# A normalised group is scaled one turn later in ScalarE's order, behind the copy of a further input group

## The chip, the cores and the metric

The kernel runs on one core of one Trainium2 chip. The metric is the device time of one execution in microseconds (us). A core has five engines that run their own instruction queues and meet at semaphores: TensorE (PE), VectorE (DVE), ScalarE (ACT), GpSimd (POOL) and SyncE (SP, which only issues transfers here). The time before is 3870.34 us, the median of three runs.

## What is computed

Two transformer layers with adaptive layer norms on x of 16 sequences x 256 tokens x 128 features, in f32. Cut to its frame, the reference is:

```python
# layer 0
h = _layernorm(x) * (1 + ca) + sa
x = x + ga * _L0_attn_ref(h, ...)        # linear attention and an MLP of 512
h = _layernorm(x) * (1 + cb) + sb
x = x + gb * _L0_ffn_ref(h, ...)         # six layers of local attention and gated MLP
# layer 1
h = _layernorm(x) * (1 + ca) + sa
x = x + ga * _L1_attn_ref(h, ...)        # causal multi-query attention with a relative bias
h = _layernorm(x) * (1 + cb) + sb
x = x + gb * _L1_ffn_ref(h, ...)         # MLP of 512
```

where `_layernorm` is `(x - m) / sqrt(v + eps)` over the 128 features, and the scales, shifts and gates (`ca`, `sa`, `ga` and so on) are one value per sequence and feature, from a small product at the start. The change touches the four lines with `_layernorm` and nothing else.

## The kernel before, in words

x is held transposed (features on partitions, `xT`, 128 x 4096), and so is the normalised result (`yT`). The program is a chain of stages with a barrier of all engines behind each. Four of the stages are calls of `layernorm_modulate`, tagged n0, n1, n2 and n3. Each works on 8 groups of 512 tokens. For one group the work goes round all engines:

- **front**, the copy in. In n1, n2 and n3 ScalarE copies the group from `xT` to `src` (L266), and TensorE transposes it into a bank of the four-deep ring `TA` (L190, four 128 x 128 transposes), so that tokens are on partitions. In n0 the input comes from memory into `src` by a transfer (L170); TensorE transposes that, and ScalarE copies `TA` to `xT` (L270).
- **stats**: VectorE takes sums (L217) and means and variances (L222); GpSimd makes `rstd` from them (L249, L251).
- **norm**: VectorE subtracts and multiplies (L229) into `xn`, two deep.
- **back**: TensorE transposes `xn` into `TB`, two banks (L197), and ScalarE applies scale and shift per sequence, in two instructions of 256 columns, into `yT` (L275). This pair on ScalarE is what is called **out** below; its semaphore is `out_done`.
- **residual**, in n2 only: VectorE adds the gated result of the stage before to `xT` (L236), and ScalarE's copy of the group waits for that.
- **split**: GpSimd makes high and low parts of the next stage's weights, beside the rest: two instructions in each of six turns in n1 (L480, L482), one in some turns of n3 (L1829 to L1839) and of n2 (L2108 to L2120).
- **swap**, in n2 only and for groups 4 to 7: TensorE multiplies two pieces of the relative bias by a matrix (L2087) into two spare banks, and ScalarE takes them out in four copies (L2098, L2099).

What sets the order is one table, `LN_ORDER`, from which every engine spells its own queue: in turn t, each engine does those of its steps that the table names, in the table's order, each for group t minus the step's lag. No engine can pass a step of its own that waits. Before, ScalarE's turn t is front of group t, then out of group t-3, then swap of group t-1; TensorE's is front t, back t-3, swap t-1; VectorE's residual t, norm t-3, stats t-1; GpSimd's stats t-1, split t-3.

The waits that matter for the change are those of the rings:

```python
ring_wait(pe, normed, u, 1, LN_RING)   # L186: front of u waits for norm of u-4
pe.wait_ge(normed, u.count(1, 1))      # L194: back of u waits for norm of u
ring_wait(pe, out_done, u, SPG)        # L195: and for out of u-2
ring_wait(dve, back_done, u, 1)        # L227: norm of u waits for back of u-2
ring_wait(act, turned, u, 1, LN_RING)  # L265: the copy of u waits for front of u-4
act.wait_ge(back_done, u.count(1, 1))  # L273: out of u waits for back of u
```

In n2, a swap product on TensorE also waits until the spare bank's copies of two products before are out, and the copies wait for the product.

Of the kernel before, what the change touches and what calls it, by code (L numbers as in the profile page):

```python
# [121 lines left out]
def ring_wait(eng, sem, grp, per, lag=2):  # L122

    if grp.at >= lag or grp.loop is not None:
        eng.wait_ge(sem, grp.count(per, per, lag))


LN_ORDER = [("residual", 0), ("front", 0), ("norm", 3), ("stats", 1), ("back", 3), ("swap", 1), ("split", 3)]
LN_RING = 4


def spelled(order, steps, n=NGRP):


    for t in range(n + max(lag for _, lag in order)):
        for name, lag in order:
            if name in steps and 0 <= t - lag < n:
                steps[name](Group(t - lag))


def layernorm_modulate(nc, tag, g, dst, scale, bias, from_dram=None, residual=None, load=None, split=None, swap=None):


    with ExitStack() as ctx:
# [13 lines left out]
        turned, stats, aggr, varp, rstd_done, normed, back_done, out_done, x_done, res_done = map(sem, (  # L158
            "turned", "stats", "aggr", "varp", "rstd_done", "normed", "back_done", "out_done", "x_done", "res_done"))
        per_src = 16 if from_dram is not None else 1  # L160
        with nc.Block() as block:
            if from_dram is not None:
                @block.sync
                def _(sp):
                    tokens = from_dram.rearrange("b (t p) f -> p (b t) f", p=128)

                    def front(u):
                        ring_wait(sp, normed, u, 1, LN_RING)
                        ring_wait(sp, turned, u, 1, LN_RING)
                        sp.dma_start(src[:, u.at % LN_RING], tokens[:, u.at * TPG:(u.at + 1) * TPG, :]).then_inc(src_ready[u.at % LN_RING], 16)  # L170
                        if load:
                            load(sp, u.at)

                    spelled(LN_ORDER, {"front": front})
            elif load:
# [6 lines left out]
            def _(pe):  # L182
# [18 lines left out]
                if swap:  # L201
                    steps["swap"] = lambda u: swap.multiply(pe, spare, u.at)
                spelled(LN_ORDER, steps)

            @block.vector
            def _(dve):
# [34 lines left out]
                if residual is not None:  # L241
                    steps["residual"] = add_residual
                spelled(LN_ORDER, steps)

            @block.gpsimd
            def _(pool):
# [8 lines left out]
                if split:  # L255
                    steps["split"] = lambda u: split(pool, u.at, out_done)
                spelled(LN_ORDER, steps)

            @block.scalar
            def _(act):  # L260
                def front(u):
                    if from_dram is None:
                        if residual is not None:
                            act.wait_ge(res_done, u.count(1, 1))
                        ring_wait(act, turned, u, 1, LN_RING)  # L265
                        nc.scalar.activation(src[:, u.at % LN_RING].rearrange("p t f -> p (t f)"), g.xT[:, u.cols()],  # L266
                                             ACT.Copy).then_inc(src_ready[u.at % LN_RING], 1)
                    else:
                        act.wait_ge(turned, u.count(1, 1))
                        nc.scalar.activation(g.xT[:, u.cols()], TA[u.at % LN_RING][:, :], ACT.Copy).then_inc(x_done, 1)  # L270

                def back(u):
                    act.wait_ge(back_done, u.count(1, 1))  # L273
                    for q in range(SPG):
                        nc.scalar.activation(dst[:, u.cols(q * SEQ, SEQ)], TB[u.par][:, q * SEQ:(q + 1) * SEQ],  # L275
                                             ACT.Identity, bias=bias[:, u.seq(q)],
                                             scale=scale[:, u.seq(q)]).then_inc(out_done, 1)

                steps = {"front": front, "back": back}
                if swap:  # L280
                    steps["swap"] = lambda u: swap.evict(act, spare, u.at)
                spelled(LN_ORDER, steps)

# [1514 lines left out]
class NetworkWeights:  # L1798
# [25 lines left out]
    def split(self, pool, n, out_done):  # L1824

        nc = self.nc
        if n == 1:
            pool.wait_ge(self.loaded, 16 * (3 + MCH))
            nc.gpsimd.tensor_tensor(self.w1p[0][:, :], self.w1[:, :], self.zero.broadcast_to((128, MLP)), ALU.add).then_inc(self.w1_split, 1)  # L1829
        if n == 2:  # L1830
            pool.wait_ge(self.w1_split, 1)
            nc.gpsimd.tensor_tensor(self.w1p[1][:, :], self.w1[:, :], self.w1p[0][:, :].bitcast(F32),
                                    ALU.subtract).then_inc(self.w1_split, 1)
        if n == 3:
            nc.gpsimd.tensor_tensor(self.w2p[0][:, :, :], self.w2[:, :, :], self.zero.unsqueeze(2).broadcast_to((128, MCH, D)),
                                    ALU.add).then_inc(self.w2_split, 1)
        if n == 4:
            pool.wait_ge(self.w2_split, 1)
            nc.gpsimd.tensor_tensor(self.w2p[1][:, :, :], self.w2[:, :, :], self.w2p[0][:, :, :].bitcast(F32),  # L1839
                                    ALU.subtract).then_inc(self.w2_split, 1)  # L1840
# [722 lines left out]
```

## Time and profile before

| | us |
|---|---|
| median of three runs (3863.09 to 3870.75) | 3870.34 |
| the profiled execution, its own time | 3875.89 |
| its span in the trace | 3874.0 |
| stage n0, first transfer to last out | 19.5 to 43.0 |
| stage n1, first copy to last out | 216.4 to 246.6 |
| stage n2, first residual to last out | 3306.1 to 3339.5 |
| stage n3, first copy to last out | 3787.0 to 3814.5 |

The four stages together are about 115 us of 3874. In rows of a timeline, the columns are start, duration, engine, line, operation, output and inputs, shapes and count of the merged instructions, and in brackets how long the engine had been idle before and what released it. PEclk, the granted TensorE clock, is given as a share of the full 2.4 GHz; 0.50 is 1.2 GHz.

### The profile page before, as it was taken

How to read it: one execution, taken by the hardware profiler on the slowest of the kernel's cores; microseconds unless marked ns; L12 is line 12 of the kernel's file. 1: busy time of each engine (PE TensorE's matmuls, PEld its weight loads, DVE VectorE, ACT ScalarE, POOL GpSimd, SP SyncE). 2: the span in 40 equal slices, each digit the busy share in tenths (PEclk: the TensorE clock that was granted, in tenths of full speed). 3: DMA queues.
4: the chain of work that ended last, by engine and by line, in shares of the span. 5: the costliest groups of instructions: out<-in, count | busy, mean ns of one | idle time of the engine just before them, and what ended most of it. 6: DMA issues, size and time to landing. Idle time of an engine off the chain costs nothing. (4 is left out here: it accounts for less than half of the span.)

```text
span 3874.0 us, 189325 instructions
## 1 busy us (share of the span) xinstructions
PE 3676.6 (95%) x70910; PEld 2945.0 (76%) x70910; DVE 3136.4 (81%) x9407; ACT 2884.3 (74%) x8517; POOL 2453.3 (63%) x2556
## 2 busy tenths in 40 slices
PE   7869999999999999999999999999999999899997
PEld 4558888688886788876888868888688886466665
DVE  7878888688887788877888878888788887666667
ACT  4758888478885788865888758888478885677775
POOL 3657777377774677756777647777377773454553
PEclk9979999999999999999999999999999999899998
DMA  1013333233332233332333323333233331100000
GB/s 48 1 52 82 80 81 83 58 81 81 81 81 71 72 82 80 82 83 58 82 81 81 89 52 80 81 81 81 60 81 81 80 81 45 36 1 0 0 0 28
DMA packets 305289, 245.99 MB, mean 63 GB/s; under 512 B 74485, under 2 KB 299860, under 8 KB 304340
## 3 DMA queue, kind: packets, MB, share of 16 engines
q1 hardware_dynamic: 305108, 243.72, 24.9%
q8 instruction: 96, 1.57, 0.2%
q14 instruction: 85, 0.70, 0.1%
HBM read 24.54 MB, written 2.12 MB: 7 GB/s over the span
## 5 line engine op out<-in xcount | busy, mean ns | idle before, releaser
L1220 POOL TENSOR_TENSOR wa_t<-wa_t,wa_rn 128x512 f32<-128x512 f32 x768 | 785.3, 1043 | 280.5 <-DVE wa_rn L1048 277.1
L880 ACT ACTIVATE wa_pb<-wa_sc,wa_nm 128x64 f32<-128x64 f32 x3072 | 670.1, 329 | 367.4 <-DVE wa_nm L1070 336.3
L1226 POOL TENSOR_TENSOR wa_t<-wa_t 128x512 f32<-128x512 f32 x384 | 496.1, 1292 | 413.2 <-DVE wa_t L1024 413.2
L1022 DVE TENSOR_TENSOR wa_t<-wa_pj,wa_ctab 128x512 f32<-128x512 f32 x768 | 528.0, 688 | 213.2 <-PE wa_ta L624 168.0
L45 PE MATMUL wa_pj<-lw_wqkv_high,wa_xhigh 128*128 128x512 f32 x1152 | 533.2, 463 | 37.4 <-DVE wa_t L1024 19.2
L863 ACT ACTIVATE wa_sq<-wa_pj 128x512 f32<-128x512 f32 x768 | 487.0, 636 | 61.5 <-PE wa_pj L47 59.5
L1235 POOL TENSOR_TENSOR wa_t<-wa_t 128x512 f32<-128x512 f32 x384 | 490.2, 1276 | 0.0
L47 PE MATMUL wa_pj<-lw_wqkv_high,wa_xlow 128*128 128x512 f32 x1152 | 461.2, 400 | 0.0
L46 PE MATMUL wa_pj<-lw_wqkv_low,wa_xhigh 128*128 128x512 f32 x1152 | 458.2, 398 | 1.2 <-issue 1.2
L1030 DVE TENSOR_REDUCE wa_raw<-wa_sq 128x16 f32<-128x1024 f32 x384 | 449.3, 1170 | 0.0
L683 PE MATMUL wa_ob<-wa_oT,lw_wo 128*128 128x128 f32 x3120 | 420.3, 278 | 3.1 <-DVE wa_on L1082 3.0
L743 PE MATMUL wa_ob<-wa_vv,wa_pT 64*32 64x65 f32 x24576 | 387.3, 227 | 26.5 <-issue 23.9
L683 PEld LDWEIGHTS wa_ob<-wa_oT,lw_wo 128*128 128x128 f32 x3120 | 383.3, 193 | 7.9 <-issue 6.2
L743 PEld LDWEIGHTS wa_ob<-wa_vv,wa_pT 64*32 64x32 f32 x24576 | 316.6, 105 | 38.3 <-issue 29.9
L2190 POOL TENSOR_TENSOR mq_pb<-mq_pb,mq_rs 128x256 f32<-128x256 f32 (+1 forms) x256 | 206.1, 826 | 219.7 <-DVE mq_rs L2335 219.7
L730 PE MATMUL wa_sc<-wa_kT,wa_qT 64*32 64x64 f32 x24576 | 329.6, 223 | 1.8 <-issue 1.6
L1024 DVE TENSOR_TENSOR wa_t<-wa_pj,wa_stab 128x256 f32<-128x256 f32 x768 | 318.9, 415 | 0.0
L1023 DVE TENSOR_TENSOR wa_t<-wa_pj,wa_stab 128x256 f32<-128x256 f32 x768 | 318.8, 415 | 0.0
L730 PEld LDWEIGHTS wa_sc<-wa_kT,wa_qT 64*32 64x32 f32 x24576 | 301.7, 105 | 2.8 <-issue 2.2
L1070 DVE TENSOR_REDUCE wa_nm<-wa_sc 128x8 f32<-128x512 f32 x384 | 265.6, 692 | 45.7 <-PE wa_sc L730 22.2
L45 PEld LDWEIGHTS wa_pj<-lw_wqkv_high,wa_xhigh 128*128 128x128 f32 x1152 | 217.6, 189 | 108.5 <-DVE wa_t L1024 31.3
L1082 DVE TENSOR_TENSOR wa_on<-wa_ob,wa_rs 128x512 f32<-128x512 f32 x384 | 261.8, 682 | 1.5
(287 smaller groups left out, 8633.4 us busy)
## 6 DMA issues: line engine op xcount, KB each, us to landing
wa_vv<-wa_vt SPq DMA_DIRECT2D x2304, 65.0 KB
wa_vv<-wa_vt SPq DMA_DIRECT2D x1152, 32.5 KB
lw_wqkv<-L_ffn_Wqkv SPq DMA_DIRECT2D x6, 1536.0 KB, 6.1
lw_xs<-yT SPq DMA_DIRECT2D x96, 64.0 KB, 1.9
lw_fs<-yT SPq DMA_DIRECT2D x48, 128.0 KB
lw_xs<-yT SPq DMA_DIRECT2D x96, 63.8 KB, 1.9
lw_fs<-yT SPq DMA_DIRECT2D x96, 63.8 KB
lw_wo<-L_ffn_Wo SPq DMA_DIRECT2D x6, 512.0 KB, 4.2
```

The lines of the kernel that those rows point to most:

```text
L45: nc.tensor.matmul(out, lhs[0], rhs[0], start=start, stop=False)
L46: nc.tensor.matmul(out, lhs[0], rhs[1], start=False, stop=False)
L47: return nc.tensor.matmul(out, lhs[1], rhs[0], start=False, stop=stop)
L683: last = nc.tensor.matmul(OB[:, 0, Y0:Y0 + 128], wo[:, PR * h + j, :], oT[:, u.tile(5), PR * h + j, :], start=(j == 0), stop=(j == PR - 1) ...
L730: last = nc.tensor.matmul(SC[q, e, p * KEYS:(p + 1) * KEYS], qT[r, u.par(2), p, q], kT[r, h2, p, k0:k0 + KEYS], start=False, stop=True, sk ...
L743: last = nc.tensor.matmul(OB[q, e, p * VW:(p + 1) * VW], pT[r, u.par(3), p, q], vv[r, u.ring(3), n, p, :], start=True, stop=True, skip_gro ...
L863: nc.scalar.activation(sq[:, j * HG:(j + 1) * HG, :], PJ[j][:, :].rearrange("p (h d) -> p h d", h=HG), ACT.Square).then_inc(s.sq_done, 1)
L880: last = nc.scalar.activation(pb[:, u.par(2), p, e, :], SC[:, e, p * KEYS:(p + 1) * KEYS], ACT.Exp, bias=nm[:, u.par(2), e, p:p + 1])
L1022: nc.vector.tensor_tensor(t1[:, b, j], x, table(ctab, slice(0, HD)), ALU.mult)
L1220: nc.gpsimd.tensor_tensor(here, here, rn[:, u.par(1), j * HG:(j + 1) * HG].unsqueeze(2).broadcast_to((128, HG, HD)), ALU.mult).then_inc(s. ...
L1226: nc.gpsimd.tensor_tensor(t1[:, b, 0], t1[:, b, 0], t2[:, b, 0], ALU.add).then_inc(s.qadd_done, 1)
L1235: nc.gpsimd.tensor_tensor(t1[:, b, 1], t1[:, b, 1], t2[:, b, 1], ALU.add).then_inc(s.kadd_done, 1)
```

## The change

Two lines: the table gets an eighth entry, `("out", 4)`, behind split, and ScalarE registers its function `back` under that name rather than under `"back"`. TensorE keeps `"back"` at lag 3.

```diff
-LN_ORDER = [("residual", 0), ("front", 0), ("norm", 3), ("stats", 1), ("back", 3), ("swap", 1), ("split", 3)]
+LN_ORDER = [("residual", 0), ("front", 0), ("norm", 3), ("stats", 1), ("back", 3), ("swap", 1), ("split", 3), ("out", 4)]
 LN_RING = 4
...
-                steps = {"front": front, "back": back}
+                steps = {"front": front, "out": back}
                 if swap:
                     steps["swap"] = lambda u: swap.evict(act, spare, u.at)
                 spelled(LN_ORDER, steps)
```

The queues of TensorE, VectorE, GpSimd and SyncE stay row for row as they were. ScalarE's turn t becomes front of t, swap of t-1, out of t-4. The first place is ScalarE in n3 (n1 is alike, and n0 too with the line L270 for L266), from the first copy on; `n_src<-xT` is the copy in, `yT<-n_tb` the out pair:

```order
 L259 UNCONDITIONAL_BRANCH
-L266 ACTIVATE n_src<-xT 128x512 x4
+L266 ACTIVATE n_src<-xT 128x512 x5
 L275 ACTIVATE yT<-n_tb,mod 128x256 x2
 L266 ACTIVATE n_src<-xT 128x512
```

Five copies stand ahead of the first out pair, where four did; from there the two alternate, and the last five pairs stand behind the last copy, where four did (x10 for x8).

The second place is ScalarE in n2, in the turns with swap; `mq_bias<-n_spare` are the copies of the relative bias. Before, from the copy of group 6 to that of group 7 and the pair behind it:

```order
L266 ACTIVATE n_src<-xT 128x512
L275 ACTIVATE yT<-n_tb,mod 128x256 x2
L2098 ACTIVATE mq_bias<-n_spare 128x2x128
L2099 ACTIVATE mq_bias<-n_spare 128x2x256
L2098 ACTIVATE mq_bias<-n_spare 128x2x128
L2099 ACTIVATE mq_bias<-n_spare 128x2x256
L266 ACTIVATE n_src<-xT 128x512
```

And now the same turn:

```order
L266 ACTIVATE n_src<-xT 128x512
L2098 ACTIVATE mq_bias<-n_spare 128x2x128
L2099 ACTIVATE mq_bias<-n_spare 128x2x256
L2098 ACTIVATE mq_bias<-n_spare 128x2x128
L2099 ACTIVATE mq_bias<-n_spare 128x2x256
L275 ACTIVATE yT<-n_tb,mod 128x256 x2
L266 ACTIVATE n_src<-xT 128x512
```

The pair moved from ahead of the four copies to behind them, and it is the pair of group 2, where it was that of group 3.

## Rows read from the trace of the kernel before

**Rows 1.** The page's first line.
```profile
span 3874.0 us, 189325 instructions
```
**Rows 2.** Timeline of ScalarE at the end of stage n0.
```profile
38.07 0.60 ACT L270 ACTIVATE xT<-n_ta 128x512 f32<-128x512 f32 x1 [1.14 <-PE n_ta L190]
38.56 2.91 ACT L275 ACTIVATE yT<-n_tb,mod 128x256 f32<-128x256 f32 x6
41.97 1.02 ACT L275 ACTIVATE yT<-n_tb,mod 128x256 f32<-128x256 f32 x2 [0.50 <-PE n_tb L197]
```
**Rows 3.** Timeline of GpSimd in stage n1, one turn of six.
```profile
234.41 0.20 POOL L249 TENSOR_TENSOR n_rstd<-n_mv,eps 128x4 f32<-128x4 f32 x1
...
236.80 1.27 POOL L482 TENSOR_TENSOR lw_wqkv_low<-lw_wqkv,lw_wqkv_high 128x512 fp32r<-128x512 f32 x1
238.03 0.20 POOL L249 TENSOR_TENSOR n_rstd<-n_mv,eps 128x4 f32<-128x4 f32 x1
```
**Rows 4.** Timeline of VectorE at the end of stage n1.
```profile
242.97 1.37 DVE L229 TENSOR_SCALAR n_xn<-n_ta,n_mv,n_rstd 128x128 f32<-128x128 f32 x4 [2.25 <-POOL n_rstd L251]
```
**Rows 5.** Timeline of ScalarE in stage n3, one turn of four.
```profile
3803.18 0.62 ACT L266 ACTIVATE n_src<-xT 128x512 f32<-128x512 f32 x1
3805.86 1.02 ACT L275 ACTIVATE yT<-n_tb,mod 128x256 f32<-128x256 f32 x2 [2.06 <-PE n_tb L197]
3806.78 0.62 ACT L266 ACTIVATE n_src<-xT 128x512 f32<-128x512 f32 x1
```
**Rows 6.** Timeline of VectorE in stage n3: stats of groups 3, 4 and 7, last norms.
```profile
3796.24 0.89 DVE L217 BATCH_NORM_STATS2 n_st<-n_ta 128x6 f32<-128x128 f32 x4
...
3798.71 0.88 DVE L217 BATCH_NORM_STATS2 n_st<-n_ta 128x6 f32<-128x128 f32 x4
...
3808.61 0.89 DVE L217 BATCH_NORM_STATS2 n_st<-n_ta 128x6 f32<-128x128 f32 x4 [1.04 <-PE n_ta L190]
...
3809.84 2.85 DVE L229 TENSOR_SCALAR n_xn<-n_ta,n_mv,n_rstd 128x128 f32<-128x128 f32 x8
```
**Rows 7.** Timeline of GpSimd in stage n3, the last `rstd`.
```profile
3810.28 1.01 POOL L251 TENSOR_TENSOR n_rstd<-n_rstd,mhalf 128x4 f32<-128x4 f32 x1
```
**Rows 8.** Timeline of ScalarE in stage n2, copies of groups 5 to 7 and the end.
```profile
3319.65 0.62 ACT L266 ACTIVATE n_src<-xT 128x512 f32<-128x512 f32 x1
...
3326.50 0.63 ACT L266 ACTIVATE n_src<-xT 128x512 f32<-128x512 f32 x1
3328.32 1.02 ACT L275 ACTIVATE yT<-n_tb,mod 128x256 f32<-128x256 f32 x2 [1.19 <-PE n_tb L197]
3329.24 0.38 ACT L2098 ACTIVATE mq_bias<-n_spare 128x256 f32<-128x256 f32 x1
...
3330.80 0.63 ACT L266 ACTIVATE n_src<-xT 128x512 f32<-128x512 f32 x1
...
3337.47 1.99 ACT L275 ACTIVATE yT<-n_tb,mod 128x256 f32<-128x256 f32 x4
```
**Rows 9.** Timeline of TensorE and VectorE in stage n2.
```profile
3327.19 0.66 PE L190 MATMUL n_ta<-ident,n_src 128*128 128x128 f32 x4 [1.48 <-ACT n_src L266]
...
3328.12 1.88 PE L2087 MATMUL n_spare<-mq_hank,mq_swap 128*128 128x512 f32 x4
...
3318.08 0.85 DVE L236 SCALAR_TENSOR_TENSOR xT<-yT,mod,xT 128x256 f32<-128x256 f32 x2
```
**Rows 10.** Line L2087 over the whole run, duration in ns min/median/max.
```profile
L2087 PE MATMUL n_spare<-mq_hank,mq_swap x16: 592/592/1057, 3322.1 to 3335.9; 128*128 128x512 f32 x16
```
**Rows 11.** Timeline of TensorE in n0, behind a wait of 2.41 us.
```profile
29.30 1.12 PE L190 MATMUL n_ta<-ident,n_src 128*128 128x128 f32 x4 [2.41 <-DMA n_src<-L_attn_x]
```
**Rows 12.** Stretches of the span: length, busy time of each engine, PEclk, DMA share, GB/s.
```profile
28.00:30.00 2.00, 0.69 (x3) 0.70 (x4) 1.96 (x14) 0.00 (x0) 1.01 (x3) 0.70 0.45 94
...
3330.00:3332.00 2.00, 0.52 (x6) 0.52 (x6) 0.45 (x2) 1.43 (x4) 1.56 (x2) 1.00 0.02 4
...
3812.00:3814.00 2.00, 0.66 (x4) 0.42 (x4) 0.68 (x3) 1.51 (x4) 0.00 (x0) 1.00 0.00 0
```

## The prediction

> **What bounds the kernel now.** I read the page first, for the size of what is touched, then the timeline of each engine through the four stages, and last the granted clock in stretches of them. The page gives a span of 3874.0 us [rows 1]; the profiled execution took 3875.89 us by its own time, 1.9 us more than the span and 5.6 us above the median of 3870.34. The four stages of `layernorm_modulate` are 115 us of that, each closed by a barrier, so what a stage gains or loses at its last out pair goes one to one into the time, and nothing done earlier inside a stage counts. Each has another bound:
>
> *n0* is held by VectorE and the loads until the end. In its tail ScalarE runs three out pairs back to back and then waits 0.50 us for the last group [rows 2]: little slack is left there.
>
> *n1* is held by GpSimd. One turn there takes 238.03 - 234.41 = 3.62 us, and no row has idle time in front of it [rows 3]. The last norm waits 2.25 us for GpSimd's `rstd`, and the last out pair follows that norm [rows 4].
>
> *n3* is held by a loop of ScalarE and TensorE: out of group u, behind it the copy of group u+4, its transposes, then the back transposes of u+1, then out of u+1. The turn is 3806.78 - 3803.18 = 3.60 us, with 2.06 us of ScalarE waiting in it [rows 5]. VectorE, when not held, needs 3798.71 - 3796.24 = 2.47 us a turn; late in the stage it waits 1.04 us a turn for TensorE [rows 6]. That n1 and n3 both show 3.6 us is chance: in n1 GpSimd's two splits a turn make it, and the loop happens to be as long.
>
> *n2* has the same loop until group 5. Then it has bias products too: 3330.80 - 3326.50 = 4.30 us from copy to copy [rows 8].
>
> **The change, part by part.** No instruction is added or removed; only ScalarE's order differs. Since nothing is added, each price is a difference in when the last out pair ends.
>
> *n0: +0.4 us.* Five pairs now stand behind the last copy in place of four. The pairs take (2.91 - 1.02) / 2 = 0.95 us each from start to start. The last copy is released by TensorE, as before. So the fifth pair starts at 38.56 + 4 x 0.95 = 42.36, against 41.97 [rows 2]. The back transposes wait for the pair of two groups before: that of group 3 ends at about 39.6, four transposes take 0.66 [rows 9], and the pair of group 5 is not due before 40.46; so for groups 6 and 7 too, some 0.2 us apart. ScalarE alone sets this. The loads do not see the change; if they did, a late one could cost some tenths more.
>
> *n1: 0.* ScalarE's and TensorE's work moves earlier, up to VectorE's norms, which wait for GpSimd. GpSimd waits for nobody in turns 4 to 8, so the last norm stays at 242.97 and the last pair where it is [rows 3, 4]. The cover is GpSimd's splits; without them this stage would behave as n3. Bounds: -0.5 and +0.5, for the clock of the last transposes.
>
> *n3: -2.5 us.* The copy of group u+4 no longer stands behind out of u, so TensorE finds its input ready and the loop is open: back transposes of u+1 need norm u+1 and out of u-1, and both are there. Next late is VectorE. From its stats of group 4 on it can keep 2.47 us a turn: stats of group 7 at 3798.71 + 3 x 2.47 = 3806.12 rather than 3808.61 [rows 6]. Its norm then waits for `rstd`, which ended 3810.28 + 1.01 = 3811.29, that is 2.68 us behind the start of those stats [rows 7]: 3808.80, and with the same 1.37 us as in n1 [rows 4] norm ends at 3810.2, where before the norms ended at 3809.84 + 2.85 = 3812.69. GpSimd has at most 1.27 us of split a turn here beside 1.3 us of `rstd`, 2.5 in all, which about fits. I take -2.5; if GpSimd is a little too long, -2.0; if the last two transposes run at the other clock, 0.5 off either way (1.12 against 0.66 us for four [rows 9, 11]).
>
> *n2: +4.9 us.* Here the pair does not only move behind the next copy, it moves behind the bias copies of its turn, and these wait for TensorE's products of the same turn. TensorE's back transposes of group t-3 stand ahead of those products and wait for out of t-5. So the pair, the copy of the next group, its transposes, the back transposes, the products and the bias copies come to stand in one line, where before the pair ran beside the products. The turn, at full clock: copy to first product 3328.12 - 3326.50 = 1.62 [rows 8, 9]. A product is two pieces, and four pieces take 1.88 us, the last 0.59 [rows 9, 10], so a piece is 0.43 from start to start and the first product is out 0.43 + 0.59 + 0.02 = 1.04 behind its start, the second 0.86 later. The second bias copy pair follows that and takes (3330.80 - 3329.24) / 2 = 0.78; the out pair takes 3329.24 - 3328.32 = 0.92 [rows 8]. Sum 1.62 + 1.04 + 0.86 + 0.78 + 0.92 = 5.22 against 4.30.
> Ahead of that, the copy of group 5 is freed from the pair and starts behind its residual, at 3318.08 + 0.85 + 0.04 = 3318.97 instead of 3319.65, which brings the turn forward by 0.68 [rows 8, 9]; but out of group 1 (0.92) now stands ahead of the copy of group 6: +0.24, at 3326.74. Copy of group 7: 3331.96. Out of group 3 starts 4.30 later, 3336.26, and is done at 3337.32; only then come back transposes of 5 and, 0.43 on, the last products; their copies start at 3338.8 and 3339.65, out of group 4 at 3340.4, and three more pairs at 0.95 behind it: the last starts at 3343.3 and ends at 3344.3, against 3337.47 + 1.99 = 3339.46 [rows 8]. That is +4.9.
>
> *The clock in n2.* In the new turn of 5.22 us TensorE works for 3328.12 - 3327.19 = 0.93 of transposes and 1.88 of products, and waits for 2.41 us, where it was 1.48 [rows 9]. Before, the clock stayed at 1.00, the 2.4 GHz level, over those waits [rows 12]. In n0 a wait of 2.41 us was followed by transposes at 1.12 us for four, and the clock of that stretch was 0.70, so it had fallen to the 1.2 GHz level [rows 11, 12]. A turn at the low level costs 2 x (1.12 - 0.66) + 4 x (1.057 - 0.592) = 2.8 us more [rows 9, 10, 11]. I take none for the forecast, since the products keep TensorE busier than n0's transposes did; one to three such turns are rivals.
> The Trainium skill (TensorE: Matmul & The Clock Gate, HAM oscillation) says that waits between short bursts throw the clock back, so that each next burst starts slow; by it the sum would have 2.8 us more per turn. The row of n0 agrees, the rows of n2 before do not yet show it.
> Stages n1 and n3 are almost all transposes, and n3's last ones ran at 1.00 [rows 12]. The same page (Part 4: PE-mode transpose) says that transposes do not raise the clock; the trace speaks against it here, and by it n2 would hang on the products alone and fall more easily.
>
> **The sum:** 0.4 + 0 + 4.9 - 2.5 = +2.8 us, or 3875.89 + 2.8 = 3878.7 for the profiled execution and 3873.1 for the median. That is 0.07%.
>
> **The rivals.**
> *A, the clock falls in one or two turns of n2* (0.20 and 0.10). For it: the longer wait and n0's row. Against: n2's turns hold 1.88 us of products each. It gives +5.6 or +8.4: 3875.9 or 3878.7, the second just past 0.2%.
> *B, the clock stays low from the first product turn of n2 to the end* (0.06). Three turns, 8.4 us: +11.2, or 3881.5, slower by 0.29%. It decides if the clock does not rise around 3326, as it did before, or falls at once. Against: the first products run without a gap, as before.
> *C, the wait for out of t-5 does not bind in n2* (0.09), because TensorE runs ahead: n2 then costs at most the 0.92 of a pair, and the net is 0.4 - 2.5 + 0.92 = -1.2 or less: 3869. Against: the queue order allows TensorE no step past back transposes.
> *D, n1 gains too* (0.03): if GpSimd's busy rows had slack that the timeline hides, six turns could fall from 3.6 towards 2.5: -6 more, 3867. Against: VectorE waits for exactly that engine.
> That the change does not do what it says is excluded: the order shows it, and only on ScalarE.
>
> **How the numbers follow.** The forecast has 0.52, the rivals the rest. What a measurement of this kernel can tell from no change is about 0.2%, 7.7 us; the three runs before alone differ by that much. Forecast, C, D and one slow turn all lie within it; slower needs B or two slow turns, and the spread of runs: 0.13. Faster by more than 7.7 us comes from no case but the spread: 0.03. The range runs from 3867 (D, or C with the spread) to 3881 (A, nearly B); the likeliest case alone, with the bounds of its terms, is 3871 to 3876.
>
> **What would show it.** In the profile of the changed kernel: in n3 stats of the last groups 2.5 us apart with no wait for TensorE, and the stage ending 2.5 us sooner against its first copy; in n1 a last pair at the same distance from the first copy, 30.2 us; in n0 five pairs in a row; in n2 out pairs behind the bias copies, copies of groups 6 and 7 5.2 us apart and TensorE waiting about 2.4 us ahead of its transposes, the stage 38 us long for 33.4. Wrong would be: a shorter n2, a wait for `rstd` gone in n1, or a difference outside these stages.

## The result, and the profile after

The changed kernel takes 3878.83 us, the median of eight runs (3873.01 to 3884.7); the kernel before takes 3870.8 us over its eight runs of the same comparison. The ratio is 1.0020, with a 95% interval of 1.0012 to 1.0029: 8.0 us slower, between 4.6 and 11.2. That is inside the range (3867 to 3881 us), well above the forecast (+2.8) and close to rival A with two slow turns (+8.4). It is just past the 0.2% that I had called the limit of what can be told.

The profiled execution after took 3873.01 us by its own time, with a span of 3871.2 us, 2.8 us *shorter* than the one before. The two spans must not be compared: the local attention between n1 and n2, which no edit touches, took 3059.5 us there and 3050.2 us here. The stages themselves can be compared, since each begins behind a barrier (one execution each; run 4 shows how far a stage can differ from one execution to the next):

| stage, from where to where | before | after | forecast | 
|---|---|---|---|
| n0, last input copy to end of last out pair | 4.92 | 6.20 | +0.4 |
| n1, first copy to end of last out pair | 30.19 | 30.18 | 0 |
| n2, the same | 32.48 | 40.49 | +4.9 |
| n3, the same | 27.45 | 25.13 | -2.5 |
| sum of differences | | +7.0 | +2.8 |

Timeline of ScalarE after, in n2, which answers to [rows 8]:

```profile
3319.35 0.65 ACT L266 ACTIVATE n_src<-xT 128x512 f32<-128x512 f32 x1
3322.46 0.39 ACT L2098 ACTIVATE mq_bias<-n_spare 128x256 f32<-128x256 f32 x1 [2.46 <-PE n_spare L2087]
...
3324.16 0.39 ACT L2098 ACTIVATE mq_bias<-n_spare 128x256 f32<-128x256 f32 x1 [0.83 <-PE n_spare L2087]
...
3324.92 1.03 ACT L275 ACTIVATE yT<-n_tb,mod 128x256 f32<-128x256 f32 x2
3325.82 0.65 ACT L266 ACTIVATE n_src<-xT 128x512 f32<-128x512 f32 x1
```

The wait has moved. Before, ScalarE waited 1.19 us in such a turn, for the back transposes. Now it waits 2.46 us and then 0.83 us for the products, and the out pair stands behind both. From copy to copy the turn is 6.47 us where it was 4.30, and where 5.22 was forecast at the high clock. TensorE in the same stretch:

```profile
3320.05 0.66 PE L190 MATMUL n_ta<-ident,n_src 128*128 128x128 f32 x4 [2.40 <-ACT n_src L266]
3320.55 0.60 PE L197 MATMUL n_tb<-ident,n_xn 128*128 128x128 f32 x4
3320.99 3.14 PE L2087 MATMUL n_spare<-mq_hank,mq_swap 128*128 128x512 f32 x4
3326.52 0.66 PE L190 MATMUL n_ta<-ident,n_src 128*128 128x128 f32 x4 [2.40 <-ACT n_src L266]
...
3331.30 0.71 PE L197 MATMUL n_tb<-ident,n_xn 128*128 128x128 f32 x4 [1.97 <-ACT yT L275]
3331.82 3.53 PE L2087 MATMUL n_spare<-mq_hank,mq_swap 128*128 128x512 f32 x4
```

The wait ahead of the transposes is 2.40 us, for a forecast of 2.41. The row of 3331.30 shows the link on which the sum rested: back transposes waiting 1.97 us for an out pair (L275). But the four pieces of the products took 3.14 us in this turn and 3.53 us in the last, where [rows 9] has 1.88. The clock fell while they ran, as stretches of the span show (length, busy time of each engine, PEclk, DMA share, GB/s):

```profile
3320.00:3322.00 2.00, 1.95 (x10) 1.41 (x11) 1.35 (x11) 0.00 (x1) 0.99 (x1) 0.87 0.00 0
3322.00:3324.00 2.00, 2.00 (x3) 0.33 (x1) 1.31 (x5) 0.87 (x2) 1.78 (x3) 0.50 0.00 0
3324.00:3326.00 2.00, 0.12 (x1) 0.00 (x0) 0.00 (x0) 1.84 (x5) 0.43 (x1) 0.78 0.01 4
3326.00:3328.00 2.00, 1.48 (x10) 1.24 (x11) 0.78 (x4) 0.47 (x1) 0.00 (x0) 1.00 0.00 0
...
3332.00:3334.00 2.00, 2.00 (x4) 0.83 (x3) 1.36 (x4) 0.23 (x1) 0.00 (x0) 0.50 0.00 0
```

0.87, 0.50, 0.78, 1.00 and again 0.50: the clock goes down to the 1.2 GHz level and up to 2.4 GHz from turn to turn. Before, it rose once, behind the first product turn (its four pieces took 3.62 us in both kernels), and then stayed up through the stage; [rows 12] has a stretch of that.

Timeline of VectorE after in n3, which answers to [rows 6]:

```profile
3795.09 0.88 DVE L217 BATCH_NORM_STATS2 n_st<-n_ta 128x6 f32<-128x128 f32 x4
...
3797.55 0.88 DVE L217 BATCH_NORM_STATS2 n_st<-n_ta 128x6 f32<-128x128 f32 x4
...
3800.01 0.88 DVE L217 BATCH_NORM_STATS2 n_st<-n_ta 128x6 f32<-128x128 f32 x4
...
3804.95 0.88 DVE L217 BATCH_NORM_STATS2 n_st<-n_ta 128x6 f32<-128x128 f32 x4
...
3807.66 1.37 DVE L229 TENSOR_SCALAR n_xn<-n_ta,n_mv,n_rstd 128x128 f32<-128x128 f32 x4 [0.17 <-POOL n_rstd L251]
```

Stats are 2.46 us apart to the end with no wait for TensorE, and the last norm waits 0.17 us for `rstd`, as worked out.

In n1 the second, third and fourth out pair come sooner after the first copy than before; the last five start 3.61 us apart, GpSimd's pace. The row that answers to [rows 4], VectorE:

```profile
244.95 1.36 DVE L229 TENSOR_SCALAR n_xn<-n_ta,n_mv,n_rstd 128x128 f32<-128x128 f32 x4 [2.24 <-POOL n_rstd L251]
```

With the first copy at 218.36 that is 26.59 us into the stage; before it was 242.97 - 216.38 = 26.59.

The tail of n0 after, ScalarE first, to be held against [rows 2], then TensorE and VectorE:

```profile
38.78 0.60 ACT L270 ACTIVATE xT<-n_ta 128x512 f32<-128x512 f32 x1 [1.73 <-PE n_ta L190]
39.27 1.93 ACT L275 ACTIVATE yT<-n_tb,mod 128x256 f32<-128x256 f32 x4
41.56 1.94 ACT L275 ACTIVATE yT<-n_tb,mod 128x256 f32<-128x256 f32 x4 [0.35 <-PE n_tb L197]
43.96 1.02 ACT L275 ACTIVATE yT<-n_tb,mod 128x256 f32<-128x256 f32 x2 [0.46 <-PE n_tb L197]
```
```profile
40.44 2.00 PE L197 MATMUL n_tb<-ident,n_xn 128*128 128x128 f32 x8 [0.84 <-ACT yT L275]
42.80 1.12 PE L197 MATMUL n_tb<-ident,n_xn 128*128 128x128 f32 x4 [0.37 <-DVE n_xn L229]
```
```profile
41.63 1.12 DVE L229 TENSOR_SCALAR n_xn<-n_src,n_mv,n_rstd 128x128 f32<-128x128 f32 x4 [0.81 <-PE n_tb L197]
```

It had been forecast that the five pairs run in one piece. They do not; there are two waits between them. Read from the end: the last pair waits for the last transposes, these for norm of group 7, this for back transposes of group 5 (L227, the ring of `xn`), and these, from 40.44, for out of group 3. The transposes took 1.12 us for four here; before they took 0.66 us in this tail.

### The profile page after: what moved, and what is told of

Same layout as the page of the kernel before. It is cut to its first block and busy times, and to the rows that moved or that the text cites. A ratio compares the mean times of both kernels' runs of the same rounds, so it can differ in the third digit from the quotient of the medians.

```text
span 3871.2 us, 189325 instructions
## 1 busy us (share of the span) xinstructions
PE 3673.9 (95%) x70910; PEld 2938.1 (76%) x70910; DVE 3133.8 (81%) x9407; ACT 2890.6 (75%) x8517; POOL 2454.3 (63%) x2556
```

## The experiments

In all kernels below the table is chosen per stage, with `OLD` as before and `NEW` as in the change:

```diff
+LN_NEW = [("residual", 0), ("front", 0), ("norm", 3), ("stats", 1), ("back", 3), ("swap", 1), ("split", 3), ("out", 4)]
+LN_OLD = [("residual", 0), ("front", 0), ("norm", 3), ("stats", 1), ("back", 3), ("out", 3), ("swap", 1), ("split", 3)]
```

Stage lengths of n1 to n3 are from the first copy to the end of the last out pair; times of kernels are medians against the kernel before on the same chip.

**1. Out at lag 4, but ahead of swap.**

```diff
-... ("back", 3), ("swap", 1), ("split", 3), ("out", 4)]
+... ("back", 3), ("out", 4), ("swap", 1), ("split", 3)]
```

> All four stages keep out at lag 4, but it stands ahead of swap in the order instead of at its end; only stage n2 differs from the change by that. My theory (in n2 the loss comes from the out pair standing behind the bias copies, which wait for TensorE's products, which stand behind back transposes that wait for an out pair): n2 goes back to 33 to 34 us from 41.4, out pairs run at once behind the copy of their turn, n3 stays at 25.1 us and n1 at 30.2; over before n0 +0.4 to +2, n2 0 to +0.5, n3 -2.3, sum 0 to -2 us. Rival 1 (lag 4 as such costs n2, since pairs pile up at the end, wherever they stand in a turn): n2 stays at 38 us or more and the kernel at +5 us. Rival 2 (the loss is outside the four stages): the kernel stays at +8 us although n2 is short.

Measured: n2 is 33.29 us, n3 24.82, n1 30.18, n0 6.20 from its last copy. The kernel: 3868.09 us, ratio 1.0000 (0.9991 to 1.0009). ScalarE's timeline, to be compared with the one above:

```profile
3321.14 0.63 ACT L266 ACTIVATE n_src<-xT 128x512 f32<-128x512 f32 x1
3321.66 1.02 ACT L275 ACTIVATE yT<-n_tb,mod 128x256 f32<-128x256 f32 x2
...
3325.43 0.63 ACT L266 ACTIVATE n_src<-xT 128x512 f32<-128x512 f32 x1
```

The pair goes out at once behind the copy, and copies are 4.29 us apart. All but 0.8 of n2's 8.0 us hangs on which side of the bias copies the pair stands; both rivals fall. With n2 back, what is left of the stages nearly cancels, and so does the kernel's time.

**2. The new order in n2 alone.** `order=LN_NEW` for n2, `LN_OLD` for the others.

> The new order in stage n2 alone, the old one in n0, n1 and n3. My theory: n2 is 38.3 us long with TensorE's clock at 1.00 throughout its product turns, 2.8 us more for each product turn at 0.50, so 38 to 44 us against 33.4; the kernel is +5 to +9 us against before, which is more than the whole change made only if the gain of n3 (2.3 us) is real. Rival 1 (n0 brings half of the loss): +4 us or less. Rival 2 (the loss is outside the stages): nothing within the stage but a few us.

Measured: n2 43.02 us, 10.5 us over the 32.48 of before (six profiles of n2 in the old order lie between 32.29 and 33.07); 3875.66 us, ratio 1.0022 (1.0013 to 1.0031), +8.5 us. Copies of groups 6 and 7 are 6.89 us apart. This one stage carries the whole loss.

**3. The same, with TensorE's waits partly filled.**

```diff
-steps["swap"] = lambda u: swap.multiply(pe, spare, u.at)
+steps["swap"] = lambda u: (swap.multiply(pe, spare, u.at), [nc.tensor.transpose(TA[(u.at + 2) % LN_RING][:, 0:D], g.ident[:, :], g.ident[:, :]) for _ in range(10 if u.at >= 4 else 0)])
```

> As the run with the new order in n2 alone, but behind the products of each of the four product turns TensorE does ten more 128x128 transposes of the identity into a bank that is free, about 1.1 us at the high clock, inside the 2.4 us for which it waits there. They add nothing that anyone reads. My theory of a loss of two parts: the waits let the clock fall, so with them partly filled the clock stays at 1.00 from the first product turn's end, every later turn is 5.2 us from copy to copy, and n2 is 38 to 39 us; the kernel +4 to +6 us against before. If the clock has no part in the loss: n2 as long as in that run, or longer by the fillers. If it is all clock: n2 back to 33 to 34 us.

Measured: n2 37.84 us; 3874.15 us, ratio 1.0014 (1.0005 to 1.0023). TensorE's timeline (L202 are the added transposes) and ScalarE's copies:

```profile
3324.52 1.88 PE L2087 MATMUL n_spare<-mq_hank,mq_swap 128*128 128x512 f32 x4
3326.24 1.25 PE L202 MATMUL n_ta<-ident 128*128 128x128 f32 x10
3328.80 0.66 PE L190 MATMUL n_ta<-ident,n_src 128*128 128x128 f32 x4 [1.30 <-ACT n_src L266]
3329.29 0.60 PE L197 MATMUL n_tb<-ident,n_xn 128*128 128x128 f32 x4
3329.73 1.88 PE L2087 MATMUL n_spare<-mq_hank,mq_swap 128*128 128x512 f32 x4
```
```profile
3322.89 0.65 ACT L266 ACTIVATE n_src<-xT 128x512 f32<-128x512 f32 x1
...
3328.10 0.65 ACT L266 ACTIVATE n_src<-xT 128x512 f32<-128x512 f32 x1
```

Products at 1.88 us in every turn but the first, a turn of 5.21 us against 5.22 forecast: more work on TensorE, and the stage is 5.2 us shorter. So of run 2's 10.5 us in n2, about half is the longer line (5.4 us, run 3 against before) and about half the clock (5.2 us, run 2 against run 3). That is read from one profile of each. The kernels' medians are only 1.5 us apart, with intervals of the ratio that overlap (1.0022 and 1.0014), so what the clock costs on average of the executions is not shown, and is likelier less than 5.2 us.

**4. The changed kernel once more.**

> The changed kernel once more, for a second look at its clock. My theory: in n2 each product turn is 5.2 us from copy to copy with the transposes at 0.66 us and the products at 1.88 us, and up to 2.8 us longer where they run at the low clock, so n2 is 37.8 to 43 us from the first copy, wherever the fall comes; n3 25 us, n1 30.2 us, n0 6.2 us from its last copy. Rival (n2's length has nothing to do with the clock): 40.5 us again with other speeds of the transposes.

Measured: n2 43.08 us, n3 24.95, n1 30.20, n0 6.20; one run of 3879.65 us. TensorE in n2:

```profile
3324.22 2.86 PE L2087 MATMUL n_spare<-mq_hank,mq_swap 128*128 128x512 f32 x4
3329.48 1.04 PE L190 MATMUL n_ta<-ident,n_src 128*128 128x128 f32 x4 [2.39 <-ACT n_src L266]
...
3331.17 2.81 PE L2087 MATMUL n_spare<-mq_hank,mq_swap 128*128 128x512 f32 x4
3335.94 0.64 PE L197 MATMUL n_tb<-ident,n_xn 128*128 128x128 f32 x4 [1.97 <-ACT yT L275]
3336.41 3.58 PE L2087 MATMUL n_spare<-mq_hank,mq_swap 128*128 128x512 f32 x4
```

The waits (2.39, 1.97) are as before, and the stage is 2.6 us longer than in the first profile of this kernel. Only half of that is the clock. From the copy of group 5 to the end of the stage it is 29.81 us, and it was 28.51; there the clock fell in three turns and not in two. The other 1.3 us lie ahead of that copy (13.27 us from the first copy, and it was 11.98), and most of them are this: GpSimd's first split starts when its weights have arrived, and here it ran beside VectorE's residual of group 5, which then took 1.69 us. In the first profile that residual took 0.85 us, and the overlap came with group 6's, off the line:

```profile
3310.71 0.85 DVE L236 SCALAR_TENSOR_TENSOR xT<-yT,mod,xT 128x256 f32<-128x256 f32 x2
```

and in this one, VectorE and GpSimd:

```profile
3313.12 1.69 DVE L236 SCALAR_TENSOR_TENSOR xT<-yT,mod,xT 128x256 f32<-128x256 f32 x2
3313.09 1.04 POOL L2108 TENSOR_TENSOR mq_wq_high<-mq_wq,zero 128x512 fp32r<-128x512 f32 x1 [1.52 <-DMA mq_bout<-L_attn_bout]
```

Runs 2 and 3 have that overlap too (13.23 and 13.16 us to the copy of group 5), so the comparison between them stands. In all three profiles of n2 in this order without fillers (40.5, 43.0, 43.1 us) the clock fell in at least two turns.

**5. The new order in n3 alone.**

> The new order in stage n3 alone. My theory: n3 is 25.1 us long, first copy to end of last out pair, against 27.45 before, VectorE's stats 2.47 us apart; the kernel gains 2.3 us, of which three rounds may not tell much. Rival (n3's length moves with the clock, not with the order): 25 to 27.5 us with turns of 3.6 us left in it.

Measured: n3 25.01 us, stats 2.46 to 2.47 us apart; 3865.41 us, ratio 0.9995 (0.9986 to 1.0004), which can't be told from 1. Over all the runs here, n3 is 26.87 to 27.48 us in the old order (eight profiles) and 24.82 to 25.18 us in the new one (five profiles).

**6. The new order in n1, with GpSimd relieved.** The first of the two splits is made by ScalarE:

```diff
-        pool.wait_ge(lw.w_loaded, 48)
-        nc.gpsimd.tensor_tensor(hi[:, here], full[:, here], zero.broadcast_to((128, WCOLS)), ALU.add).then_inc(lw.w_first, 1)
+        act.wait_ge(lw.w_loaded, 48)
+        nc.scalar.activation(hi[:, here], full[:, here], ACT.Copy).then_inc(lw.w_first, 1)
```

as a step `("high", 3)` of ScalarE, behind back and, in this order, ahead of out; GpSimd's second split then waits for it.

> Stage n1 alone has the new order, and GpSimd's cover there is halved: the first of its two splits a turn (adding zero and rounding) is made by ScalarE as a copy, behind the front copy of its turn. n0, n2 and n3 have the old order. My theory (n1 showed nothing because GpSimd's 3.6 us a turn hid the opened loop): GpSimd needs 2.5 us a turn now, the loop is open, and n1 falls from 30.2 to 24.5 us; the kernel gains 5.6 us. Rival (the loop of ScalarE and TensorE holds n1 whatever GpSimd does): n1 stays above 29 us.

Measured: n1 24.49 us; 3862.29 us, ratio 0.9985 (0.9976 to 0.9994), -5.8 us. GpSimd's timeline, one turn:

```profile
232.39 0.20 POOL L249 TENSOR_TENSOR n_rstd<-n_mv,eps 128x4 f32<-128x4 f32 x1
...
233.64 1.27 POOL L491 TENSOR_TENSOR lw_wqkv_low<-lw_wqkv,lw_wqkv_high 128x512 fp32r<-128x512 f32 x1
234.87 0.19 POOL L249 TENSOR_TENSOR n_rstd<-n_mv,eps 128x4 f32<-128x4 f32 x1
```

2.48 us a turn, where [rows 3] has 3.62: with the cover gone the opened loop is worth 5.7 us in n1.

**7. The same relief, in the old order.** `("out", 3)` ahead of `("high", 3)`.

> As the run with the new order in n1 and the split's first half on ScalarE, but with the old order in n1 too. My theory: with out ahead of the next copy the loop is closed, and the extra copy on ScalarE stands in it: about 4.15 us a turn, n1 31.6 us long against 30.2, the kernel +1.5 us. Rival (relieving GpSimd is what gains, the order has no part in it): n1 at 25 to 27 us here too.

Measured: n1 30.92 us, 3869.21 us, ratio 1.0004 (0.9994 to 1.0013). ScalarE:

```profile
232.53 1.02 ACT L275 ACTIVATE yT<-n_tb,mod 128x256 f32<-128x256 f32 x2 [2.06 <-PE n_tb L197]
233.44 0.62 ACT L482 ACTIVATE lw_wqkv_high<-lw_wqkv 128x512 fp32r<-128x512 f32 x1
...
236.65 1.02 ACT L275 ACTIVATE yT<-n_tb,mod 128x256 f32<-128x256 f32 x2 [2.06 <-PE n_tb L197]
```

4.12 us a turn, and the same 2.06 us of waiting in it. Relief and order are worth nothing apart and 5.7 us together.

**8. In n2, the bias copies a turn later too.** ScalarE takes the products of a turn out in the next one:

```diff
-... ("back", 3), ("swap", 1), ("split", 3), ("out", 4)]
+... ("back", 3), ("out", 4), ("swap", 1), ("unswap", 2), ("split", 3)]
...
-                    steps["swap"] = lambda u: swap.evict(act, spare, u.at)
+                    steps["unswap"] = lambda u: swap.evict(act, spare, u.at)
```

> In stage n2 alone: out at lag 4 ahead of the bias copies, and the bias copies on ScalarE at lag 2, one turn behind TensorE's products, so that they never wait for products of the same turn. Others old. My theory of one long line in n2: with the bias copies out of it too the stage is 29 to 31 us from the first copy, against 32.4 before and 40.5 with the change, and the kernel gains 2 to 4 us. Rival (ScalarE's and TensorE's work as such fills the product turns): n2 stays at 32 us or more.

Measured: n2 29.30 us, 3863.81 us, ratio 0.9987 (0.9978 to 0.9996), -5 us, where the stage gives -3.2 and the interval reaches from -8.5 to -1.5. Copies of groups 5, 6 and 7 are 3.26 and 3.25 us apart, at VectorE's pace.

**9. The new order in n0 alone.**

> The new order in stage n0 alone. From the last input copy to the end of the last out pair: 4.9 us before and in three runs with the old order there, 6.2 us in both runs with the new one, where the transposes of the tail ran at 1.12 us for four. My corrected theory: the back transposes of group 5 wait for out of 3, norm of 7 for those, and the last two transposes and the pair for that, so the stage's tail depends on the transposes: 5.3 us if they take 0.66 us, 6.2 us if 1.12 us. Rival (ScalarE's five pairs alone, as forecast): 5.3 us at either.

Measured: 6.19 us from the last copy, with transposes at 1.12 us for four (one execution, 3872.56 us, which says nothing at this size). The low clock alone does not make it: in five of the runs with the old order in n0 (2, 3, 5, 6 and 7) the last input's transposes also took 1.11 or 1.12 us, and the tail was 4.83 to 4.96 us all the same. In run 2, for example, TensorE's rows are

```profile
37.57 1.11 PE L190 MATMUL n_ta<-ident,n_src 128*128 128x128 f32 x4 [1.80 <-DMA n_src<-L_attn_x]
38.48 1.91 PE L197 MATMUL n_tb<-ident,n_xn 128*128 128x128 f32 x8
```

Old order and slow transposes, and no wait between groups 4 and 5; and behind these the transposes of groups 6 and 7 got faster again, down to 0.66 us in runs 3 and 6. In all four profiles of the new order without fillers, the transposes of groups 5 to 7 took 1.12 us to the end of the stage, even in run 4, where the last input's had taken 0.66 us. So the slow tail goes with the new order here; that the new order causes it is not shown. How the old order does with a slow tail to the end, no run shows, so how much of the 1.3 us is the order's and how much the clock's is bounded only by the next run.

**10. The same, with fillers in n0's waits.**

```diff
+LN_RING = 4; FILL = {2: 2, 3: 6, 4: 3}
...
                     last.then_inc(back_done, 1)
+                    if from_dram is not None and u.at in FILL:
+                        pe.wait_ge(x_done, 5)
+                        for t in range(FILL[u.at]):
+                            nc.tensor.transpose(TA[0][:, 0:D], g.ident[:, :], g.ident[:, :])
```

> The new order in n0 alone, with 2, 6 and 3 transposes of the identity into a free bank behind the back transposes of groups 2, 3 and 4, inside TensorE's waits, so that its clock may be high in the tail. If the last transposes then take 0.66 us for four: my corrected chain (last copy, out of 3, back of 5, norm of 7, back of 7, out of 7) gives 0.5 + 1.05 + 0.7 + 1.15 + 0.7 + 1.05 = 5.2 to 5.3 us from the last copy, against 6.2 in four runs with slow ones and 4.9 with the old order. If they stay at 1.12 us: 6.2 again, and the fast case stays unseen. Rival (the tail is 6.2 us whatever the transposes take): 6.2 at 0.66 us too.

Measured: 5.28 us (one execution, 3869.97 us). ScalarE, where L274 and L279 are the lines L270 and L275 of before:

```profile
37.74 0.60 ACT L274 ACTIVATE xT<-n_ta 128x512 f32<-128x512 f32 x1 [1.36 <-PE n_ta L190]
38.24 4.78 ACT L279 ACTIVATE yT<-n_tb,mod 128x256 f32<-128x256 f32 x10
```

With the transposes at 0.66 us the five pairs run in one piece, as the forecast had them, and the tail is 0.4 us longer than in the old order. The last two transposes were just in time, so both the chain and ScalarE's own work give that figure.

**11. What the runs favour in each stage, together.** n0 as before, n1 as in run 6, n2 as in run 8, n3 as in the change.

> Each stage with what the runs so far favour: n0 the old order; n1 the new one with the split's first half on ScalarE; n2 out at lag 4 ahead of the bias copies and these at lag 2; n3 the new order. If the stages add up, as they must with a barrier behind each: n1 24.5, n2 29.3, n3 25.0 us, so -5.7 - 3.1 - 2.3 = -11 us against before, some 0.29%. If a stage's length leans on the one before it (the clock that is handed over): -7 to -9 us.

Measured: 3857.82 us against 3867.8, ratio 0.9974 (0.9964 to 0.9983), 10 us faster than before and 18 us faster than the change by the two ratios. n1 24.55, n2 29.06, n3 25.18 us: the stages give 5.6 + 3.4 + 2.3 = 11.3 us, and the interval reaches from 6.6 to 13.9, so they add up within it.

## Why the prediction was right in kind and short in size

- *n1: 0.* Right to 0.01 us, and for the reason given: run 6 takes the cover away and the gain appears (24.49 us).
- *n3: -2.5.* -2.3 in the first profile, about -2.1 between the medians of all profiles. VectorE is next late, as forecast.
- *n2: +4.9, the line.* The mechanism was right link by link: the pair behind the bias copies (run 1 undoes just that), the turn of 5.22 us (5.21 in run 3), the wait of 2.41 us (2.40), and ahead of it a copy of group 5 that comes 0.69 us sooner after the first copy, for 0.68 forecast (in runs 2, 3 and 4 VectorE's slow residual hides that). The line alone measures 5.4 us in run 3, 4.9 of them behind the copy of group 5, where the forecast had 5.5; its first products took 2.95 us for 3.62 before, which is the difference.
- *n2, the clock.* Here is the step that failed: "I take none for the forecast, since the products keep TensorE busier than n0's transposes did". n0's row with a wait of 2.41 us and a fallen clock [rows 11, 12] was the nearest evidence for a wait that I had worked out at 2.41 us, and I set it aside for an argument with no row behind it. Clock falls came in all three profiles, and from the copy of group 5 on the stage is 3.8 to 5.1 us longer than run 3. Rival A had the right mechanism, at a chance of 0.30 that looks low now, but not the right sizes: the falls came in two or three turns, and such a turn is 1.3 to 1.7 us longer than run 3's 5.21 (6.47, 6.89 and 6.88 us), not 2.8, because the low level held for a part of the turn only. The Trainium skill cited there (TensorE: Matmul & The Clock Gate, HAM oscillation) describes such a clock for bursts that are shorter than the waits between them. In the trace of the change PEclk is 1.00 and 0.50 in turn, with products at 1.88 and 3.53 us, although TensorE's 2.8 us of work were longer than its wait of 2.40; and it is not as the page has it that the next burst starts slow, since the transposes ahead of the slow products still took 0.66 us (in run 4 they took 1.04).
- *n0: +0.4.* "ScalarE alone sets this" holds at the high clock (5.28 us in run 10) and not at the low one, where back of 5 and norm of 7 come into the line: +1.3 in all four profiles without fillers. I checked the ring on TensorE with 0.66 us only, though the trace of before had n0 at both speeds, and left out the ring of `xn` on VectorE (L227).
- *The sum.* With 1.3 + 0 + 8.0 to 10.6 - 2.3 the stages give +7.0 to +9.6; the kernels' comparison gives +8.0, between 4.6 and 11.2. Nothing outside the stages is needed. That the result lies so near rival A's +8.4 is in part luck: A's price of a slow turn was too high, and n0, which A left at +0.4, was too low. Since both clock terms lie on the same side, the likeliest case's own range (3871 to 3876) was too low, and the wide one held. The chance of 0.13 for more than 0.2% slower looks too small, with a result that lies on that line.

## What to carry to other kernels

Take a step of engine A that engine B will wait for (here the out pair). In A's written order it must not stand behind a step that itself waits for B's work of the same turn (here the bias copies): then the two engines take turns and no longer overlap. Follow the line across both queues, step by step. A loop that is opened pays only where nothing else needs the same time; in n1, relief of GpSimd and the new order were worth nothing apart and 5.7 us together. And price each new wait of TensorE with the clock at its low level, if any row shows it falling behind a wait of that length.

## What the runs showed of the hardware

Giving TensorE ten more transposes a turn made a stage 5.2 us shorter, because its other instructions then ran at the high clock (1.88 us for four pieces of the products in each of the last three turns). The fillers are transposes, as are the ones in run 10 that kept n0's tail fast; the Trainium skill (TensorE: Matmul & The Clock Gate, Part 4: PE-mode transpose) says that transposes do not count as work for the clock, beside figures for bf16. For the f32 transposes here, these two runs speak against it.

In n0 the profile's clock and the durations do not always agree. After, the stretch of the tail reads

```profile
40.00:42.00 2.00, 1.56 (x7) 1.39 (x8) 1.19 (x6) 1.65 (x4) 0.35 (x1) 1.00 0.00 0
```

a granted clock of 1.00, while the transposes in it took 1.12 us for four, as they do at 0.50 elsewhere. In run 9 the same stretch, with the same durations, reads 0.50. There I went by the durations.

The local attention between n1 and n2 took 3059.5 us in the profile before and 3050.2 us in the one after, with the same instructions. A difference of a few microseconds in this kernel can be read from stages in a trace, and hardly from spans.
